# Membership table and turned routing weights held in 128 partitions instead of 41

## What is computed

```
logits = x @ gate_w
scores = jax.nn.softmax(logits, axis=-1)
topk_w, topk_idx = jax.lax.top_k(scores, K)            # K = 2 of E = 8 experts
comb = jnp.zeros((T, E)).at[jnp.arange(T)[:, None], topk_idx].add(topk_w)
g = jax.nn.silu(jnp.einsum('td,edh->teh', x, w_gate)) * jnp.einsum('td,edh->teh', x, w_up)
routed = jnp.einsum('teh,ehd,te->td', g, w_down, comb)
shared = jax.nn.silu(x @ sw_gate) * (x @ sw_up) @ sw_down
```

## Time and profile before

| | |
|---|---|
| median of 3 runs | 1310.9 us (1307.07, 1310.9, 1310.99) |
| profiled execution | 1307.69 us |
| its span, first to last instruction | 1306.0 us |
| mean granted TensorE clock | 0.963 of full |
| busy: PE, PEld, DVE, ACT, POOL | 1199.6, 1044.7, 884.8, 732.5, 538.6 us |
| DMA | 56.04 MB |

### The profile page before, as it was taken

One profiled execution on the slowest core, in us unless ns is written; L12 is line 12 of the kernel. 1 busy time (PEld: TensorE's weight loads), 2 busy tenths in 40 slices (PEclk: granted clock), 3 DMA queues, 4 the chain that ended last, 5 costly groups with the idle time before them and its releaser, 6 DMA issues. The chain is left out here.

```text
span 1306.0 us, 27038 instructions
## 1 busy us (share of the span) xinstructions
PE 1199.6 (92%) x9589; PEld 1044.7 (80%) x9589; DVE 884.8 (68%) x1829; ACT 732.5 (56%) x1285; POOL 538.6 (41%) x559
## 2 busy tenths in 40 slices
PE   5999999999879999999999999999999876997798
PEld 4888888889758888888788887888878776785586
DVE  5666656566657887878887788778886465555554
ACT  4656556556545666576665666666656433442443
POOL 2423232232225363553545535445364063562242
PEclk9999999999988999999999999999999967997799
DMA  4211111110031111011110111101000070022000
GB/s 144 69 42 56 39 34 53 39 39 1 2 90 53 48 48 48 1 47 47 47 47 0 47 47 34 60 0 47 0 1 1 1 246 20 2 115 86 1 1 15
DMA packets 38795, 56.04 MB, mean 43 GB/s; under 512 B 3106, under 2 KB 37202, under 8 KB 38226
## 3 DMA queue, kind: packets, MB, share of 16 engines
q1 hardware_dynamic: 37922, 54.23, 13.1%
q10 hardware_dynamic: 816, 1.05, 0.3%
HBM read 54.81 MB, written 0.46 MB: 42 GB/s over the span
## 5 line engine op out<-in xcount | busy, mean ns | idle before, releaser
L1118 POOL TENSOR_TENSOR att_sq<-att_work,att_sq 128x500 fp32r<-128x500 f32 x90 | 119.8, 1331 | 159.7 <-DVE att_sq L1018 159.7
L1122 POOL TENSOR_TENSOR attention_kk<-att_work,attention_kk 128x500 fp32r<-128x500 f32 x90 | 122.1, 1357 | 153.3 <-DVE attention_kk L1026 153.3
L102 PE MATMUL att_csum<-att_pT,att_cn 125*128 125x448 f32 x384 | 156.3, 407 | 5.1 <-DVE att_pT L1067 4.4
L944 ACT ACTIVATE att_pr<-att_pr,att_nmx 112x1500 f32<-112x1500 f32 (+1 forms) x96 | 108.5, 1130 | 72.4 <-DVE att_nmx L1055 72.4
L104 PE MATMUL att_csum<-att_pT,att_cn 125*128 125x448 f32 x384 | 141.1, 367 | 0.0
L103 PE MATMUL att_csum<-att_pT,att_cn 125*128 125x448 f32 x384 | 140.0, 365 | 0.0
L535 DVE SCALAR_TENSOR_TENSOR attention_kk<-kvs_keys_ps,kvs_bk,attention_kk 64x500 fp32r<-64x500 f32 x96 | 70.8, 738 | 91.7 <-ACT attention_kk L419 90.1
L1067 DVE TENSOR_TENSOR att_pT<-att_ring,att_pT 125x448 fp32r<-125x448 f32 x192 | 118.3, 617 | 21.7 <-ACT att_pT L960 21.5
L1052 DVE TENSOR_SCALAR_CACHE_REDUCE att_pr<-att_ring 112x500 f32<-112x500 f32 x192 | 121.8, 675 | 6.4 <-PE att_ring L104 5.0
L290 PE MATMUL kvs_feat<-kvs_f,attention_kk 128*125 128x256 f32 x768 | 113.0, 284 | 10.9 <-DVE kvs_kp L607 10.1
L877 PEld LDWEIGHTS att_ring<-all_ident,att_pr 112*125 112x125 f32 x768 | 110.9, 190 | 14.4 <-ACT att_pr L944 2.2
(11 more groups left out here) (279 smaller groups left out, 3276.9 us busy)
## 6 DMA issues: line engine op xcount, KB each, us to landing
attention_raw_t<-in_ctxT SPq DMA_DIRECT2D x45, 500.0 KB, 4.0
att_raw_n<-in_ctx SPq DMA_DIRECT2D x16, 750.0 KB
tail_gate_w<-in_gate SPq DMA_DIRECT2D x1, 2112.0 KB, 8.1
tail_up_w<-in_up SPq DMA_DIRECT2D x1, 2112.0 KB, 13.9
kvs_raw_q<-in_wq SPq DMA_DIRECT2D x8, 256.0 KB, 4.0
tail_wo_raw<-in_wo SPq DMA_DIRECT2D x4, 512.0 KB, 6.9
tail_down_w<-in_down SPq DMA_DIRECT2D x1, 2048.0 KB, 18.0
tail_gate_w<-in_gate SPq DMA_DIRECT2D x1, 1760.0 KB, 12.0
```

What stands on the lines that cost most here:

```text
L102: nc.tensor.matmul(out, w_lo, x_hi, start=start, stop=False, skip_group_check=True)
L944: nc.scalar.activation(pr[:, j, keys], pr[:, j, keys], ACT.Exp, scale=-1.0, bias=nmx[:, j:j + 1], accum_out=z[:, 4 * u + j, c:c + 1]).then ...
L1118: nc.gpsimd.tensor_tensor(sq[1][:, i % 2, :], work[:, i % 2, :], sq[0][:, i % 2, :].bitcast(F32), ALU.subtract).then_inc(sq_lo, 1)
L1122: nc.gpsimd.tensor_tensor(kk[:, c, 2 + gi, :], work[:, i % 2, :], kk[:, c, gi, :].bitcast(F32), ALU.subtract).then_inc(k_lo, 1)
```

## The change

Both tiles get 128 partitions. The matmul of line 1524 takes the whole tiles, and so contracts over 128 partitions. The memsets of lines 2104 and 2107 take whole tiles as well and clear 128 partitions each. Nothing else writes partitions 41 to 127, which stay zero.

```
-        combT = p.sb("combT", [LO + E + 1, NTOK], F32R)
-        member = p.sb("member", [LO + E + 1, units], F32R)
+        combT = p.sb("combT", [128, NTOK], F32R)
+        member = p.sb("member", [128, units], F32R)
```

## The result

| | before | changed |
|---|---|---|
| median | 1310.62 us (6 runs, 1307.07 to 1311.38) | 1299.24 us (6 runs, 1295.38 to 1301.24) |
| ratio of the runs | | 0.9915, 95% interval 0.9897 to 0.9934 |
| span of the profiled execution | 1306.0 us | 1293.7 us |
| mean granted clock | 0.963 | 0.967 |

The change makes the kernel faster by 0.85%, 11.1 us of 1310.6 (interval 8.7 to 13.5). The forecast was 1300.3 us, a gain of 8.9. The order of work on TensorE, VectorE and ScalarE is the same; on GpSimd the two memsets alone differ.

A forecast was written before the change was run, and what follows sets the result against it. TensorE was taken to bound the kernel. From a base of 1309.2 us, 8.5 us for 23 regular spreads plus 0.4 for the opening spreads, memsets zero, made a gain of 8.9 and 1300.3 us; range 1296.4 to 1306.

The forecast's parts named there:

- The bound: Whole kernel: TensorE, busy for 92% of the span, limits it and stays the limit after the change.
- the excess of 0.37: Regular blocks: three steps around a spread take 0.90 us where 0.53 is usual; all 0.37 us was expected to go.
- the rival of one side only: Line 1524: only the way in (1306.9 us) or only the way out (1302.8 us) is due to the rows; chance 0.07.
- The count: Regular spreads that pay: 9 in moe0 and 14 in moe1, 23 x 0.37 = 8.5 us.
- The fifteenth stall: Moe1's last spread, n = 16: gains nothing, since narrow(16) waits for VectorE anyway.
- The mechanism: Line 1524: the 41-row operand keeps loads from being pulled ahead going in and coming out; 128 rows remove the 0.37 us.
- the first rule: Line 1524: a load costs by columns, not contraction rows, so no gain, 1309.2 us; the no-change rival had chance 0.09.
- The pair of spreads: Spreads 0 and 1 of each mixture: gain between nothing and 0.36 us each, half taken, 0.4 in all.
- the two rows: Memsets, lines 2104 and 2107: clearings of 41x2112 (1.86 us) and 128x2176 (1.92 us) imply cost 0.0 for 128 partitions.
- The rival of the readout's clock: Readout: earlier work moves where the clock falls, 1.5 us allowed either way; slower clock or other loss, chance 0.04.
- The full price of 10 us: Readout: if all of it fell to half clock, 10 us lost, giving 1310.3 us.
- The base: Time of the kernel before from which the gain was subtracted: mean of four executions, 1309.2 us.

The follow-up runs named there:

- the second profile: The changed kernel, unedited, timed and profiled again beside the kernel before: median 1298.86 us against 1308.65, ratio 0.992.
- the one with all fillings: Changed kernel plus unread matmuls in the waits before the second layer norm, both spreads 0 and two turns of the third layer norm: 1288.89 us, ratio 0.9857.

## Why the prediction was right

The bound was read rightly: a regular block went from 4.44 to 4.07 us, exactly the excess of 0.37, and PE stayed the bound. The steps of the way in and of the way out are both usual now, so the rival of one side only is out.

The count held. 9 x 0.37 with moe0's pair of spreads were 3.5; measured are 3.55. 14 x 0.37 with moe1's pair were 5.4; measured are 5.5 in the profile with the same clock. The fifteenth stall indeed paid nothing. From the last matmul of widen(16) to narrow(16) it is 1299.57 - 1295.77 = 3.80 us before and 1287.24 - 1283.43 = 3.81 now; what the stall gave up has become idle time of PE ahead of narrow(16), 0.41 us. The starts of that last matmul, before and changed:

```profile
1295.77 0.36 PE L104 MATMUL tail_bank<-tail_xn,tail_wide 128*64 128x448 f32 x1
```
```profile
1283.43 0.36 PE L104 MATMUL tail_bank<-tail_xn,tail_wide 128*64 128x448 f32 x1
```

The mechanism was right, with more certainty than the trace of before could give. There the excess was known, not its cause; it stood against a rule, and the choice fell on the row count because the waits were long met. 64 against 65 rows shows that it is the row count. Both rules of the Trainium skill agree with the runs, each in its place. The load's own duration goes by its columns ("TensorE: Matmul & The Clock Gate", section "LDWEIGHTS (loading the stationary operand)"): 181 ns for 9 rows and 188 for 128, and 134 ns for the one load of 64 columns. That a change of tiling mode drains TensorE is what "TensorEngine Tiling (Array Packing)", section "Key Properties", of the Trainium skill says. It gives no price. The runs fit it: 0.37 us for going in and out of 64 rows or fewer, shared by neighbours of the same kind. That such a change is what happens inside the engine is the reading, not a row of the trace. As a rival the first rule would have led to no change, because it prices the load and not the order in which loads may start.

The pair of spreads was taken at 0.2 for each mixture. The two stages leave it room of 3.55 - 3.33 = 0.2 and 5.48 - 5.18 = 0.3. It can be read directly as well. From spread 0 to spread 2 moe0 took 1121.27 - 1116.51 = 4.76 us and takes 1120.48 - 1115.99 = 4.49, of which 0.10 is the way into spread 2, so the pair gave 0.17; the pair alone takes 0.50 us now (1116.49 - 1115.99), not the 0.41 that the prediction took as usual. The same two starts in moe1, in the second profile, leave 0.21. Spread 2 of moe0, before, then spreads 0 and 2, changed:

```profile
1121.27 0.46 PE L1524 MATMUL tail_bank<-tail_combT,tail_member 41*128 41x448 f32 x1
```
```profile
1115.99 0.67 PE L1524 MATMUL tail_bank<-tail_combT,tail_member 128*128 128x448 f32 x2 [2.32 <-DVE tail_combT L1681]
...
1120.48 0.37 PE L1524 MATMUL tail_bank<-tail_combT,tail_member 128*128 128x448 f32 x1
```

The memsets cost nothing, as the two rows said.

The rival of the readout's clock had the place right and the size and the sign open: in the profile after it was 2.5 us in favour, in the second profile nothing. I gave it 1.5 us either way, which was too little: between kernels of this study (the one with all fillings aside) the readout moved from 38.2 to 43.1 us, -2.5 to +2.3 against before. The full price of 10 us was never met. The measured gain, 11.1 (8.7 to 13.5) and 10.5 (8.2 to 12.7), holds the 9.0 of the stages in both intervals, near the lower ends. The start of the tail, ahead of all that the change touches, stood anywhere from 1045.7 to 1050.7 us in the profiles of the study, and that with the clock is enough to make up the rest. That it does so wasn't shown.

That the forecast time came so near, 1300.3 against 1299.24, is in part luck. The base was the mean of four executions, 1309.2, and six runs gave a median of 1310.62, 1.4 above it; the measured gain was 2.2 above the forecast one. The two gaps cancel in part.

## What to carry to other kernels

Read the starts of matmuls and of their loads, not their durations: a lone matmul whose load starts with it instead of a step ahead costs more than its row shows. Here a lone matmul that contracted over 64 rows or fewer (9, 41 and 64 were tried) between matmuls of 128 cost 0.37 us of TensorE time more, and holding its operands in more than 64 partitions, the rest of them zero, took that away at no cost. Where that can't be done, two such matmuls side by side share one stall, but the later start of the first can cost part of it again. When a gain is under one per cent, compare stages cut at the same instructions: the granted clock elsewhere gave or took 2.5 us here, in two kernels the same in both profiles and in a third not.

## What the runs showed of the hardware

- The stall is a step function of the rows: 7.4 to 7.6 us of "issue" before line 1524's loads with 9, 41 and 64 rows, none with 65, 96 and 128.
- The columns make no such difference here: the last block's spread with 64 columns has no idle load time with 128, 96 or 65 rows, and 0.35 us with 64.
- The readout, with the same instructions, took 38.2 to 38.5, 40.8 to 40.9, 41.5, 42.2 and 43.1 us as the granted clock fell for more or less of it; kernels that differ in nothing but the row count ahead of it met different values (40.8 with 64 rows, 43.1 with 9), and two profiles of one kernel agreed to 0.1 us in two cases and differed by 2.6 in a third.
- Unread matmuls in waits of 2.3 to 5.6 us bought some 8 us by the ratios (0.9857 against 0.9920), with the clock at 1.00 over the whole readout where it was 0.81 and 0.71 in the changed kernel's two profiles; in one wait alone, that of 5.6 us, they bought nothing (0.9933). Which of them the clock answers to isn't known.
